# Expert loop of a mixture-of-experts layer: the order of TensorE, ScalarE and VectorE work per block, and where TensorE reads its expert numbers

## What is computed

```python
g = jnp.einsum('ech,ehi->eci', xg, w_gate)      # xg: rows of the tokens, per expert
u = jnp.einsum('ech,ehi->eci', xg, w_up)
y = jnp.einsum('eci,eih->ech', jax.nn.silu(g) * u, w_down).reshape(E * C, H)
out = jnp.zeros((T + 1, H), x.dtype).at[t_slot].add(w_slot[:, None] * y)
```

## Time and profile before

| | us |
|---|---|
| runs (3): lowest, median, highest | 624.79, 627.1, 627.71 |
| span of the profiled execution, first to last instruction | 719.4 |
| of it before 355 us: attention, choice of experts | 355 |
| 355 to 389: tables, fill of the queues, first loads | 34 |
| 389 to 658: expert loop | 269 |
| 658 to 719.4: sum per token, normalisation, store | 61.4 |
| busy over the span: PE, PEld, DVE, ACT, POOL | 563.9, 414.4, 368.4, 330.1, 390.5 |

### The profile page before, as it was taken

The page is one execution under the profiler, slowest core; times in us unless marked ns, Lnnn a source line. Parts: engine busy times, 40 slices in busy tenths (PEclk is TensorE's granted clock), DMA queues, the critical chain, the costliest instruction groups (busy, mean ns, idle before and its releaser), DMA issues.

```text
span 719.4 us, 17476 instructions
## 1 busy us (share of the span) xinstructions
PE 563.9 (78%) x5097; PEld 414.4 (58%) x5098; DVE 368.4 (51%) x1527; ACT 330.1 (46%) x1204; POOL 390.5 (54%) x599
## 2 busy tenths in 40 slices
PE   3768787888878888888306889988998888985995
PEld 2445454544555554444105777777777776774884
DVE  1537566666677566666402444444444444443453
ACT  2445555455455455456003555555555554553012
POOL 5443445545544455545551666766666666665432
PEclk9789999999999899999556999999999999998899
DMA  9999996111111111112285554555555454554994
GB/s 206 277 275 365 342 339 231 69 59 73 68 50 64 55 73 73 65 66 74 99 308 182 155 165 150 160 156 167 152 164 159 143 157 142 164 160 148 425 418 145
DMA packets 83069, 121.31 MB, mean 169 GB/s; under 512 B 13779, under 2 KB 72669, under 8 KB 80992
## 3 DMA queue, kind: packets, MB, share of 16 engines
q1 hardware_dynamic: 64128, 78.46, 36.3%
q0 software_dynamic: 14016, 38.44, 14.7%
q10 hardware_dynamic: 4896, 4.03, 1.7%
HBM read 56.07 MB, written 69.01 MB: 174 GB/s over the span
## 4 chain that ended last, share of the span: by engine, by line
PE 54%; issue 12%; ACT 12%; DVE 9%; DMA 6%; ACTq 3%; POOL 2%; SPq 1%; another core or an unknown queue 0%; DVEq 0%; POOLq 0%
PE bank L793 14%; PE bank L809 9%; ACT pr L870 7%; PE bank L611 5%; PE bank L785 5%; PE bank L601 4%; PE bank L803 3%; PE bank L661 3%; DMA out<-fin 3%; PE bank L744 2%; DMA wall<-results 2%; DVE nmax L1024 2%; PE bank L619 2%; ACTq L296 1%; DVE tg L1218 1%
## 5 line engine op out<-in xcount | busy, mean ns | idle before, releaser
L556 POOL DMA_INDIRECT results<-ys,wcol x152 | 150.1, 988 | 25.8 <-POOL pscrap L545 22.0
L530 POOL DMA_INDIRECT queues<-x,xidx x128 | 129.1, 1009 | 36.9 <-issue 36.5
L793 PE MATMUL bank<-wall,xtT 128*128 x616 | 127.1, 330 | 0.7 <-issue 0.7
L870 ACT ACTIVATE pr<-bank,nmax 128x128 f32<-128x128 f32 x256 | 90.9, 370 | 29.1 <-DVE nmax L1024 29.1
L1218 DVE SCALAR_TENSOR_TENSOR tg<-th,bank 128x96 f32<-128x96 f32 x154 | 39.1, 254 | 125.3 <-ACT th L957 96.9
L793 PEld LDWEIGHTS bank<-wall,xtT 128*128 128x128 f32 x616 | 98.4, 194 | 1.4 <-issue 1.3
L963 ACT ACTIVATE ys<-bank,wcol 128x256 f32<-128x256 f32 x152 | 71.9, 473 | 54.6 <-PE bank L809 36.6
L809 PE MATMUL bank<-wall,hT 96*128 x304 | 94.5, 392 | 0.0
L785 PE MATMUL bank<-ident,xt 128*128 128x128 f32 x310 | 63.3, 286 | 35.4 <-DMA xt<-queues 24.1
L785 PEld LDWEIGHTS bank<-ident,xt 128*128 128x128 f32 x310 | 59.0, 197 | 49.9 <-DMA xt<-queues 25.1
L876 ACT COPY prT<-bank 128x512 f32<-128x512 f32 x64 | 38.5, 601 | 88.9 <-PE bank L611 86.2
(11 more groups left out here) (178 smaller groups left out, 947.2 us busy)
## 6 DMA issues: line engine op xcount, KB each, us to landing
xt<-queues SPq DMA_DIRECT2D x162, 160.0 KB
results<-zeros SPq DMA_DIRECT2D x16, 1024.0 KB
wall<-results SPq DMA_DIRECT2D x16, 1024.0 KB, 12.7
queues<-zeros SPq DMA_DIRECT2D x32, 160.0 KB, 4.9
wall<-in_L_ffn_w_gate SPq DMA_DIRECT2D x4, 768.0 KB
wall<-in_L_ffn_w_up SPq DMA_DIRECT2D x4, 768.0 KB
wall<-in_L_ffn_w_down SPq DMA_DIRECT2D x4, 768.0 KB
results<-ys,wcol POOLq DMA_INDIRECT x152
```

Source lines behind the costliest of these rows:

```text
L530: pool.indirect_dma_start(xg, bass.IndirectOffsetOnAxis(ap=xidx[:, par, k:k + 1], axis=0), x2[:, par, :], None, bounds_check=last_row, oob ...
L556: pool.indirect_dma_start(yr, bass.IndirectOffsetOnAxis(ap=wcol[:, u, 1:2], axis=0), ys[:, u, :], None, bounds_check=last_y, oob_is_err=Fa ...
L793: ins = pe.matmul(bank[2 + u % 2][:, 0:2 * INTER].rearrange("p (g i) -> p g i", g=2), xtT[:, u % 2, kk, :], wall[:, bass.ds(e, GU)].rearrange(
L870: ins = act.activation(pr[:, g % 2, q, :], pS[g % 2][:, q * P:(q + 1) * P], ACT.Exp, bias=nmax[:, 4 * g + q:4 * g + q + 1], accum_out=den[ ...
```

## The change

A constant `HALF = UN // 2` is added. The order per engine and block becomes: PE down of t, row turn of t + 5, turn of t + 2, gate/up of t + 4; ACT y of t, copy of t + 5, tanh of t + 4; DVE copy of t + 2, weights of t + 3, gate of t + 4. The work before the loop is filled up accordingly. PE's register load of eight at the head of the round becomes two loads of four, behind the second and the sixth block; eight values are carried into the next round in registers (`down_regs`, `gate_regs`), by eight moves at the end of the round. DVE's load of eight stands behind the copy of its first block. SP's and POOL's loops are untouched, as are buffers and banks.

```diff
@@ -809,24 +810,44 @@
                 pe.matmul(bank[6 + u % 2][:, 0:D], hT[:, u % 2, :], wall[0:INTER, bass.ds(e, WX)][:, GU:WX],
                           start=True, stop=True).then_inc(peF["y"], 1)
 
-            for t in range(3):
-                block_T(t, t, 0)
-            last_two = [nc.alloc_register(ET.PE, f"last_two{u}") for u in range(2)]
-            carried = [bass.RuntimeValue.of_register_unchecked(r).with_bounds(min_val=0, max_val=(NE - 1) * WX) for r in last_two]
-            for t, e in zip((0, 1), neighbours(ET.PE, tab_g[0:1, LEAD:UN], (NE - 1) * WX)):
-                pe.reg_mov(last_two[t], e)
-                gu(t, t, e)
+            def kept_registers(name, values):
+
+                regs = [nc.alloc_register(ET.PE, f"{name}{k}") for k in range(HALF)]
+                for r, v in zip(regs, values):
+                    pe.reg_mov(r, v)
+                return regs, [bass.RuntimeValue.of_register_unchecked(r).with_bounds(min_val=0, max_val=(NE - 1) * WX)
+                              for r in regs]
+
+            def experts_of(first):
+
+                return neighbours(ET.PE, tab_g[0:1, bass.ds(first, HALF)], (NE - 1) * WX)
+
+            down_regs, down_e = kept_registers("down_e", experts_of(LEAD))
+            gate_regs, gate_e = kept_registers("gate_e", experts_of(LEAD + HALF))
+            block_T(0, 0, 0)
+            block_T(1, 1, 0)
+            gu(0, 0, down_e[0])
+            block_T(2, 2, 0)
+            gu(1, 1, down_e[1])
+            block_T(3, 3, 0)
             turn_h(0, 0)
+            gu(2, 2, down_e[2])
+            block_T(4, 4, 0)
+            turn_h(1, 1)
+            gu(3, 3, down_e[3])
             with pe.Fori(0, rounds) as j:
-                e = neighbours(ET.PE, tab_g[0:1, bass.ds(j * UN + UN, UN)], (NE - 1) * WX)
                 for u in range(UN):
                     t = j * UN + u
-                    block_T(t + 3, u + 3, j)
-                    gu(t + 2, u, e[u])
-                    turn_h(t + 1, u + 1)
-                    down(t, u, e[u - 2] if u >= 2 else carried[u])
-                for u in range(2):
-                    pe.reg_mov(last_two[u], e[UN - 2 + u])
+                    down(t, u, down_e[u] if u < HALF else gate_e[u - HALF])
+                    block_T(t + 5, u + 5, j)
+                    turn_h(t + 2, u + 2)
+                    gu(t + 4, u + 4, gate_e[u] if u < HALF else later_e[u - HALF])
+                    if u == 1:
+                        later_e = experts_of(j * UN + (LEAD + UN))
+                    if u == UN - 3:
+                        coming_e = experts_of(j * UN + (LEAD + UN + HALF))
+                for r, v in zip(down_regs + gate_regs, later_e + coming_e):
+                    pe.reg_mov(r, v)
 
             for b in range(NB):
                 ps = bank[b % 8]
@@ -966,16 +987,16 @@
             for k in range(2):
 
                 act.copy(spare[0:1, k:k + 1], tab_n[0:1, 0:1]).then_inc(actF["y"], 1)
-            for t in range(3):
-                block_T(t, t)
-            for t in range(2):
+            block_T(0, 0)
+            for t in range(4):
+                block_T(t + 1, t + 1)
                 tanh(t, t)
             with act.Fori(0, rounds) as j:
                 for u in range(UN):
                     t = j * UN + u
-                    block_T(t + 3, u + 3)
-                    tanh(t + 2, u)
                     y(t, u)
+                    block_T(t + 5, u + 5)
+                    tanh(t + 4, u + 4)
 
             b = 0
             for c, n in enumerate(LAST):
@@ -1226,18 +1247,21 @@
                 dve.wait_ge(peF["hT"], t + 1)
                 dve.tensor_copy(hT[:, u % 2, :], bank[4 + u % 2][0:INTER, 0:P]).then_inc(dveF["hT"], 1)
 
-            for t, column in zip((0, 1), neighbours(ET.DVE, tab_w[0:1, 0:UN], D + NE - 1)[LEAD:]):
+            for t, column in zip(range(3), neighbours(ET.DVE, tab_w[0:1, LEAD:LEAD + 3], D + NE - 1)):
                 weights(t, t, 0, column)
+            gate(0, 0)
+            gate(1, 1)
             for t in range(2):
-                gate(t, t)
-            h_T(0, 0)
+                h_T(t, t)
+                gate(t + 2, t + 2)
             with dve.Fori(0, rounds) as j:
-                columns = neighbours(ET.DVE, tab_w[0:1, bass.ds(j * UN + UN, UN)], D + NE - 1)
                 for u in range(UN):
                     t = j * UN + u
-                    weights(t + 2, u + 2, j, columns[u])
-                    gate(t + 2, u)
-                    h_T(t + 1, u + 1)
+                    h_T(t + 2, u + 2)
+                    if u == 0:
+                        columns = neighbours(ET.DVE, tab_w[0:1, bass.ds(j * UN + (LEAD + 3), UN)], D + NE - 1)
+                    weights(t + 3, u + 3, j, columns[u])
+                    gate(t + 4, u + 4)
 
             for u in range(UN):
                 dve.wait_ge(xt_in[u], rounds * 16 + (32 if u < 2 else 16))
```

More of the change, by code:

```diff
@@ L32 @@
 LEAD = UN - 2
+HALF = UN // 2
 IDLE = 2 * UN + 2
```

## The result

The change made the kernel slower. The median went from 626.9 us (624.8 to 627.7) to 635.95 us (635.4 to 637.2): the ratio is 1.016, with an interval from 1.013 to 1.018. The forecast was 612. Of the profiled execution, 633.8 us lie between the first and the last instruction, and the time of that run is 635.9, so 2.1 us lie around the span.

The account below looks back on a forecast made before the run. PE bounds the expert loop, losing time at each round's head. 19 x (0.85 - 0.1) = 14.3 us, less 0.5 in the prologue, ACT's pauses at nothing, said as 15: 627.1 to 612 us, own range 607 to 620, overall 597 to 626.

Parts of the forecast that it names:

- four lie between: 0.6 us: PE's two mid-round loads of four values: 0.6 us each, sequencer spending 0.5 us a round more, hidden, cost taken as 0.
- 0.6 us once a round against 0.85 of reserve of hg: nothing: DVE's table read moved behind hT: 0.6 us once a round, covered by hg being ready 0.85 us early, so no cost.
- Idle before down in the third and seventh block: Sign in the new profile that the prediction is wrong: PE's register loads of four are not hidden.
- The waits of the turn for hg: PE's turns waiting for hg in the loop, 18.3 us over 24 times; shrinking under half would show the prediction right.
- the head: Start of each expert-loop round, where PE idles for its sequencer's branch and load of eight: 0.85 us a round, 16 us.
- The head's moves: Eight register moves instead of two at PE's loop head: cost 0 to 0.4 us a round, taken as 0.1.
- The lead: How far PE's sequencer runs ahead of PE in the new order: about 1.3 us, hiding some 0.9, 0.3 to spare.
- The bound of 0.72 us a round: Upper bound for both PE loads of four together if the sequencer's only lead is gate/up's own 0.65 us.
- ACT's pauses: Late starts of th every four blocks in the first profile, one costing 1.36 us; counted at nothing in the likeliest case.
- Rivals 1 and 4: ACT's pauses are real in timed runs: partly absorbed, 607 us (chance 0.28), or wholly absorbed, 577 us (chance 0.03).
- Rival 2: PE's sequencer doesn't get ahead, so the head's gain is spent again on loads and head: 627 us, chance 0.10.
- Rival 3: Slower: no lead and eight single moves on PE, 1.78 us a round against 0.85: 645 us; milder 633; chance 0.09.

Follow-up runs that it names:

- e2: The changed kernel with PE's table stored two entries higher, so its two loads of four start at multiples of 16 bytes: 632.39 us, ratio 1.011 to before.
- e3: The changed kernel with both tables shifted, DVE's one entry lower and PE's two entries higher, so all loads are aligned: 608.95 us, ratio 0.973 to before.
- e1: The changed kernel with DVE's table stored one entry lower, so its load of eight starts at a multiple of 32 bytes: 617.85 us, ratio 0.988 to before.
- e0: The kernel before the change, unedited, profiled a second time: 624.59 us, span 622.9.
- e6: The changed kernel with both tables aligned, but PE's eight values read by one load at the head of the round: 615.75 us, ratio 0.985 to before.
- e4: The kernel before the change with only DVE's table stored one entry higher, 4 bytes past a multiple of 16: 640.49 us, ratio 1.024.
- e5: The kernel before the change with only PE's table stored one entry higher, so its load of eight starts misaligned: 657.84 us, ratio 1.051.
- e7: The kernel before the change, its order kept, with PE's values read by two aligned loads of four in mid-turn: 617.69 us, ratio 0.988.

## Why the prediction was wrong, point by point

**The step that failed is the price of a register load**, and it failed on both engines for one reason: the price depends on the byte at which the load starts, and the prediction had it depend on the number of values alone.
- PE, "four lie between: 0.6 us". The number was put between a load of two (0.557) and one of eight (0.66), as if the load had a fixed part and a small slope. Measured are 1.02 us in after, and 0.36 in e2 and e3, neither of them near 0.6. The row of two values starts at entry 6, 24 bytes in, the eight at a multiple of 32: the first was a dear load and the second a cheap one, so nothing lay between them. The difference of the starts was to be seen in the code.
- DVE, "0.6 us once a round against 0.85 of reserve of hg: nothing". This is the dearest term of all, 1.00 us a round, 18 us by e1. 0.6 was right for the row of before (0.598 in e0) but not for the shifted start: 2.14. With the register steps behind it, DVE stands still for 2.3 to 2.4 us. The working for the block shown above: DVE loses 0.22 before hT and 2.33 before weights, and the 0.57 that it waits for th in other blocks (445.33) goes against that, so hg is 1.98 us late. The turn starts 0.87 late, on a PE that was 0.20 late itself, so 0.91 us was covered. The reserve itself, 0.85, was thus sized rightly; 0.87 and the restart of 0.17 are the 1.0 that PE loses. The load of 0.77 and the same steps, 0.9 us together at most, leave no trace in e1 and e3.
- The place in the rule of the Trainium skill (Runtime: NRT & Kernel Launch, section Instruction fetch mechanics) was read the wrong way round. About 200 ns a register was set aside because eight values had taken 0.66; it is nearly right for the loads of after, 0.26 and 0.27 us a value, and wrong for the aligned ones, 0.07 to 0.10. The prices by that rule, 0.8 for four and 1.6 for eight, would have asked what becomes of hg behind a load of 1.6 on DVE. The prediction weighed the rule for PE alone.
- The sign was on the list. Idle before down in the third and seventh block was named as what would show the loads not hidden, and it came, 38 times (9.1 us). For DVE's load no sign was named. The waits of the turn for hg were to fall under half of 18.3 us; they are 12.0 us, for another reason than in the first profile.

**Right:**
- The pace of 1.42 us a block as the floor of PE, and the head as the one loss that is certain: 0.9 a round against 0.85. The head's moves, taken at 0.1 in a range from 0 to 0.4, cost nothing: one instruction of 0.17 us, and in e3 the head's blocks last 1.42.
- The lead. In the new order the sequencer hides a load of 1.02 us but for 0.2, and one of 0.36 wholly. Of 0.6 it was said that 0.3 would be to spare; 1.02 - 0.20, some 0.8 us, is what it can hide. The bound of 0.72 us a round was above the 0.41 that came.
- That ACT's pauses are not in the timed runs, that the refills of xt and the scatters stay covered (no DMA wait in the waits of the loop), that POOL follows, and that the prologue costs within 1 us (the first down starts at 330.2 us of the span, 329.5 before).
- The sum without the failed term. Its own terms, 14.3 less 0.5 in the prologue, give 13.8 us and 613.3; the text rounded that up to 15 and 612. e3, where the loads cost what the sum took them at, nothing, is 608.95. Of the 4.4 us between them, 2.7 are the head and its load, which gave back 0.89 us a round instead of 0.75 (19 x 0.14); the rest is within the spread of the runs of before.

**The rivals.** Rivals 1 and 4 needed ACT's pauses and fall with e0. Rival 2 had no lead at all, and falls: of loads of 1.02 us PE loses 0.41 a round in after and 0.47 in e1 (11.86 against 11.39), and nothing of loads of 0.36 in e3. Rival 3 had the sign (slower; 645, in a milder form 633) but the wrong cause: it took away the lead and priced single moves on PE's sequencer, while 1.00 of 1.41 us came from DVE's, and the moves cost nothing. That its milder form lies near the measured 635.95 is luck. The forecast of the profile's span, 719.4 to about 700, says nothing, since the 719.4 held over 90 us that no timed run has; it stands at 633.8 against 622.9.

## What to carry to other kernels

When an edit moves the place from which registers are loaded, work out the byte address of each load and shift the table so that every load starts at a multiple of 16 bytes (for eight values only multiples of 32 were tried): here that turned +1.6% into -2.7% with no instruction more. Before taking a price between two rows of one instruction, check that the rows agree in everything but the size. And when an engine's own load or wait moves into mid-stream, price it for each engine that does it, not only for the one that carries the loop.

## What the runs showed of the hardware

The price of a register load from a table on the chip, by its start (median ns; for the loads of two the fastest of the group, which is the one in the prologue):

| values | start, bytes past a multiple of 16 | ns | from |
|---|---|---|---|
| 8 | 0 | 598 on DVE at its head, 777 in mid-stream; 621 and 592 on PE | e0, e3, e6 |
| 8 | 4 | 2141 and 2056 on DVE, 2170 on PE | after, e4, e5 |
| 4 | 0 | 356 and 336 on PE | e3, e7 |
| 4 | 8 | 1024 on PE | after |
| 2 | 8 and 12 | 556 and 555 on PE | e0, e5 |

Off the multiple of 16 the price is 0.26 to 0.28 us a value at each of three sizes; on it, 0.30 to 0.36 us for each four values (0.39 for DVE's eight in mid-stream). It looks as if an aligned load moved 16 bytes at a time and another one value at a time, but that is a reading of these five rows; no run looked inside the load. That a load crosses a multiple of 32 bytes is not what makes it dear: of PE's two loads in after, the one at 8j + 14 crosses such a multiple and the one at 8j + 18 does not, and both take 1.02 to 1.03 us. Every second start in e3 and e7 is 16 bytes past a multiple of 32, and all are cheap, so 16 is enough for a load of four; for eight values only multiples of 32 were tried. The prices are those in the loop. The first loads, at 302 to 307 us, while DMA was busy 0.77 of the time (294 to 322 us), cost more, and the start counts there too: eight values 1.79 us aligned (e0) and 6.72 off (e4), four values 1.14 and 0.96 aligned (e2), 3.39 and 3.48 off (after). PE was waiting for its first rows then, so they cost the kernel nothing; whether the DMA made them dear was not tested. Why DVE's aligned load takes 0.60 us at the loop's head and 0.77 in mid-stream stays open. The Trainium skill (DMA: Bandwidth & Descriptors, section Latency and other measured facts, the row of the `tensor_load` floor) gives about 600 ns as the least that such a load costs: the aligned eight agree (592 to 621), the aligned four, at 336 to 361 ns, are well below it.
